# Seven quadrant products in place of eight in a second square layer: tiles 13 to 15 of a feed-forward and state-space kernel

## Chip, cores and metric

One core of one Trainium2 chip. The metric is the device time of one execution in microseconds, the median of the runs taken: 1422.49 us of 3 runs (1422.36 to 1422.56) for the kernel before. Lower is better.

## The reference, cut to what matters

`x` is 4 x 1024 tokens of 256 features. The feed-forward part runs twice, once before and once after the state-space part (a long convolution by transforms, an exact GELU and a projection):

```python
def ffn(x):                                     # weights are ternary: -1, 0, 1
    h = silu(tlin(x, w1_w, w1_s)) * tlin(x, w2_w, w2_s)      # 256 -> 1024
    h = gelu(tlin(h, h1_w, h1_s), approximate=False)         # 1024 -> 1024
    h = gelu(tlin(h, h2_w, h2_s), approximate=False)         # 1024 -> 1024
    return tlin(h, w3_w, w3_s)                               # 1024 -> 256
x = x + 0.5 * ffn(layernorm(x))
x = x + state_space(layernorm(x))
x = x + 0.5 * ffn(layernorm(x))
```

`tlin(x, w, s)` is `x @ w.T * s`, with one scale per output feature.

## The kernel before, in words

**Tiles.** The tokens go in tiles T of 512 (`TOK`); 8 tiles are the first feed-forward, T = 8 to 15 the second (`ALL` = 16). A hidden activation is [128 partitions, `KH` = 8 blocks, 512 tokens]; block k holds 128 of the 1024 features. An fp32 activation goes into TensorE as two fp32r parts, a rounded high part and the rest, so each product is made twice, with the same weight block, and summed in PSUM: exact enough for fp32, since the ternary weights are exact.

**Stages of one tile.** Steps are numbered k = 0 to 23 (`PER_U`). k = 0 to 7 (called m): layer one. `layer_one` (L1382 on) makes two products of 4 matmuls, into banks 2(m%2) and 2(m%2)+1; ScalarE's `hidden` (L498, L511) takes the SiLU of the first into one of three slots of `act_o`; VectorE's `gate` (L1246) multiplies it with the second product from PSUM, ScalarE's `gated_high` (L518) rounds the high part and VectorE's `gated_low` (L1251) makes the low part, into `hid_a_hi` and `hid_a_lo`. The second product of m waits for gate(m-2) (`s_gate`), as it overwrites the bank. k = 8 to 15: first square layer, `product` (L1362) with 16 matmuls of 512 columns a block, h1 by `hid_a`, into bank k%4. The first of these blocks waits for each low part (`s_glo`) as it comes to it. ScalarE takes the GELU (L511), VectorE's `split` (L1258, L1260) makes high and low parts in `hid_b_hi`, `hid_b_lo`. k = 16 to 23: second square layer, the same with h2, from `hid_b` into `hid_a`. Then the transposes of the next tile's normalised input (L1338), `layer_three` with the tokens as stationary operand and w3 (256 columns) moving, 64 matmuls (L1451), or `layer_three_last` (L1464) for tile 15, which lets VectorE and the stores follow one block of 128 tokens after the other. VectorE scales and adds (L1318, L1322; L1326, L1328 in the last tile).

**Order.** Every engine has its own instruction stream, written out in this order and tied by semaphores; there is no scheduler. Beside a step k each engine does other work where the schedule says so: `prepare` (taps of the convolution, tiles 0 to 3), `spectral` (the convolution, tiles 4 to 12), `norms` (the layer norm of the next tile; k = 12 and 13 in tiles 13 to 15). The convolution's buffers `zb`, `wb`, `fb`, `tt`, `ks` (from offset Z0) are used last in tile 12; its last batch of `x2` is stored from `wb` at the start of tile 13 (`store_batch`). SyncE issues all DMAs. `load_next` loads the next tile into `gz` after the last low part of layer one, `load_residual` the residual into `xin`.

**Branch.** Should a weight not fit fp32r, another path with fp32 is taken: in tile 0 VectorE ors all weights' bits (L1224), folds and sums them, and TensorE's queue loads the result (`flag`, L1608) and branches over two copies of the whole program. Five blocks of tile 0 are made ahead of the branch (`hidden_ahead`, L1434, L1436) but for their last matmul, which stands behind it (`hidden_end`, L1440).

**Alignment.** Weights and activations start on lines of 512 bytes, w3 64 bytes ahead of one:

```python
LAST += (LINE - 64 - base - LAST) % LINE
w3, FRONT = zone(LAST, ("w3", [P, KH, D], F32R))
```

## Time and profile before

| what | value |
|---|---|
| median of 3 runs | 1422.49 us (1422.36 to 1422.56) |
| profiled execution: span from first to last instruction | 1420.9 us |
| TensorE matmul busy | 1415.5 us (100%) |
| TensorE weight load busy (beside it) | 1164.5 us (82%) |
| VectorE busy | 986.1 us (69%) |
| ScalarE busy | 478.9 us (34%) |
| GpSimd busy | 48.8 us (3%) |
| DMA | 80.28 MB, mean 56 GB/s |
| granted TensorE clock | 1.00 (2.4 GHz) |
| chain that ended last | TensorE 97%, of it L1362 80%, L1451 8% |

How to read it: the span is one profiled execution, its rest to the median (1.6 us) is start and end outside the instructions. A share is that engine's busy time over the span. Matmuls are pipelined: one of 512 columns is listed with 390 ns, but the next starts 227 ns later, so the pace is read from where rows start and not from their lengths. In the timeline a row is: start, length, engine, line, operation, output <- inputs, count, and in brackets how long the engine was idle before it and what released it.

### The profile page before, as it was taken

To read this page: it belongs to the slowest core of one execution; us is meant where nothing else is said; L and a number is where in the kernel's file an instruction comes from. 1 tells how busy PE (TensorE), PEld (TensorE's weight loads), DVE (VectorE), ACT (ScalarE), POOL (GpSimd) and SP (SyncE) were. 2 spreads that over 40 slices of the span, in tenths; PEclk is the share of its full clock that TensorE was granted. 3 is DMA by queue.
4 is the path that set the end of the run, shared out by engine and by line. 5 is a ranking of instruction groups with operands and counts; after the bars stand their busy time and mean duration, and the time that the engine had idled before them with its cause. 6 is when DMAs were issued, how large, how long until landed. Compare 5 with 4: busy or idle time off the path is not lost.

```text
span 1420.9 us, 17300 instructions
## 1 busy us (share of the span) xinstructions
PE 1415.5 (100%) x6923; PEld 1164.5 (82%) x6923; DVE 986.1 (69%) x1742; ACT 478.9 (34%) x724; POOL 48.8 (3%) x43
## 2 busy tenths in 40 slices
PE   9999999999999999999999999999999999999999
PEld 4888888888878888788787888878878788888887
DVE  7877778675878888758888577784777755354433
ACT  5524342523425124232232332422424223141321
POOL 0000000000000000010000100001000010000000
PEclk9999999999999999999999999999999999999999
DMA  9001000012023111131210312112120112010000
GB/s 365 23 5 40 16 30 30 19 42 67 35 76 145 49 58 60 42 104 60 75 60 12 134 45 74 43 33 100 60 74 15 60 41 74 1 45 0 30 1 16
DMA packets 54434, 80.28 MB, mean 56 GB/s; under 512 B 2768, under 2 KB 46160, under 8 KB 53072
## 3 DMA queue, kind: packets, MB, share of 16 engines
q1 hardware_dynamic: 54352, 79.15, 16.4%
q8 instruction: 56, 0.92, 0.3%
q14 instruction: 26, 0.21, 0.0%
HBM read 57.12 MB, written 22.02 MB: 56 GB/s over the span
## 4 chain that ended last, share of the span: by engine, by line
PE 97%; issue 1%; DMA 1%; DVE 0%; SPq 0%
PE ps L1362 80%; PE ps L1451 8%; PE ps L1502 3%; PE ps L1555 2%; PE ps L1338 1%; PE ps L1434 1%; DMA raws<-in_weights 1%; PE ps L1436 1%; PE ps L1496 1%; PE ps L1497 1%; PE ps L1464 1%; PE ps L1545 0%; PE ps L1479 0%; DVE hid_a_lo L1251 0%; SPq L320 0%
## 5 line engine op out<-in xcount | busy, mean ns | idle before, releaser
L511 ACT ACTIVATE act_o<-ps,scales 128x512 f32<-128x512 f32 x384 | 264.5, 689 | 858.8 <-PE ps L1362 856.8
L1362 PE MATMUL ps<-hid_b_hi,h 128*128 128x512 f32 x1024 | 401.4, 392 | 0.0
L1362 PE MATMUL ps<-hid_b_lo,h 128*128 128x512 f32 x1024 | 398.6, 389 | 0.0
L1362 PE MATMUL ps<-hid_a_hi,h 128*128 128x512 f32 x984 | 386.9, 393 | 0.0
L1362 PE MATMUL ps<-hid_a_lo,h 128*128 128x512 f32 x984 | 383.0, 389 | 0.0
L1362 PEld LDWEIGHTS ps<-hid_b_hi,h 128*128 128x128 f32 x1024 | 192.2, 188 | 41.2 <-issue 1.2
L1362 PEld LDWEIGHTS ps<-hid_b_lo,h 128*128 128x128 f32 x1024 | 192.2, 188 | 40.7 <-issue 1.2
L1362 PEld LDWEIGHTS ps<-hid_a_hi,h 128*128 128x128 f32 x984 | 184.7, 188 | 40.5 <-issue 2.2
L1362 PEld LDWEIGHTS ps<-hid_a_lo,h 128*128 128x128 f32 x984 | 184.7, 188 | 40.2 <-issue 2.2
L1362 PE MATMUL ps<-hid_b_hi,w 128*128 128x512 f32 x480 | 187.2, 390 | 0.0
L1362 PE MATMUL ps<-hid_b_lo,w 128*128 128x512 f32 x480 | 186.8, 389 | 0.0
L1258 DVE CAST hid_b_hi<-act_o 128x512 fp32r<-128x512 f32 x128 | 54.4, 425 | 133.5 <-ACT act_o L511 132.8
L1258 DVE CAST hid_a_hi<-act_o 128x512 fp32r<-128x512 f32 x128 | 56.6, 442 | 126.7 <-ACT act_o L511 126.4
L1246 DVE SCALAR_TENSOR_TENSOR gz<-ps,scales,act_o 128x512 f32<-128x512 f32 x128 | 96.0, 750 | 47.0 <-PE ps L1362 44.4
L1451 PE MATMUL ps<-w,hid_a_hi 128*128 128x256 f32 x480 | 111.3, 279 | 0.0
L1451 PE MATMUL ps<-w,hid_a_lo 128*128 128x256 f32 x480 | 110.0, 277 | 0.0
L1362 PEld LDWEIGHTS ps<-hid_b_hi,w 128*128 128x128 f32 x480 | 90.1, 188 | 18.6 <-DVE gz L1318 0.3
L1362 PEld LDWEIGHTS ps<-hid_b_lo,w 128*128 128x128 f32 x480 | 90.1, 188 | 18.2
L1260 DVE TENSOR_TENSOR hid_b_lo<-act_o,hid_b_hi 128x512 fp32r<-128x512 f32 x128 | 88.7, 693 | 4.4
L1260 DVE TENSOR_TENSOR hid_a_lo<-act_o,hid_a_hi 128x512 fp32r<-128x512 f32 x128 | 88.6, 692 | 4.4
L1451 PEld LDWEIGHTS ps<-w,hid_a_lo 128*128 128x128 f32 x480 | 90.2, 188 | 0.0
L1451 PEld LDWEIGHTS ps<-w,hid_a_hi 128*128 128x128 f32 x480 | 90.2, 188 | 0.0
(275 smaller groups left out, 1277.6 us busy)
## 6 DMA issues: line engine op xcount, KB each, us to landing
ks<-k_d SPq DMA_DIRECT2D x32, 512.0 KB, 3.8
raws<-in_weights SPq DMA_DIRECT2D x9, 1024.0 KB, 13.7
xin<-in_x SPq DMA_DIRECT2D x8, 512.0 KB, 3.8
x_d<-xin SPq DMA_DIRECT2D x8, 512.0 KB, 2.8
z_d<-xin SPq DMA_DIRECT2D x8, 512.0 KB, 2.8
zb<-z_d SPq DMA_DIRECT2D x8, 512.0 KB, 4.9
wb<-x_d SPq DMA_DIRECT2D x8, 512.0 KB, 4.2
x_d<-wb SPq DMA_DIRECT2D x8, 512.0 KB, 3.5
```

The source lines that it names most:

```text
L511: A(act_o[:, k % ACT_SLOTS], bank(source), func, scale=scale).then_inc(s_act, 1)
L1246: V.scalar_tensor_tensor(gated[:, m % 2], bank(2 * (m % 2) + 1), scales[:, 1, m:m + 1], act_o[:, m % ACT_SLOTS], ALU.mult, ALU.mult).then_ ...
L1258: V.tensor_copy(hi[:, k % KH], source).then_inc(s_hi, 1)
L1260: V.tensor_tensor(lo[:, k % KH], source, hi[:, k % KH].bitcast(F32), ALU.subtract).then_inc(s_split, 1)
L1338: last = nc.tensor.transpose(ps[:, k, j * P:(j + 1) * P], gz[:, j, k * P:(k + 1) * P], ident[:, :])
L1362: last = MM(o, weight[:, k, cols].bitcast(dt), part[:, k].bitcast(dt), start=(k == 0 and i == 0), stop=(k == n - 1 and i == len(act_) - 1))
L1434: MM(bank(bank_of(0, k)), weight[:, kk, cols], hi[:, kk], start=kk == 0, stop=False)
L1436: MM(bank(bank_of(0, k)), weight[:, kk, cols], lo[:, kk], start=False, stop=False)
L1451: last = MM(o, part[:, k, j * P:(j + 1) * P].bitcast(dt), w3[:, k].bitcast(dt), start=(k == 0 and i == 0), stop=(k == KH - 1 and i == 1))
L1464: last = MM(ps[:, 4 + j, 0:D], part[:, k, j * P:(j + 1) * P].bitcast(dt), w3[:, k].bitcast(dt), start=(k == 0 and i == 0), stop=(k == KH - ...
L1502: last = MM(bank(o), tables[:, table_], flat(x), start=True, stop=True)
L1555: last = MM(o, ga[:, k, u * P:(u + 1) * P], wt[:, k], start=(k == 0), stop=(k == KD - 1))
```

## The change

In tiles 13 to 15 (`seven(T)`) the second square layer is made by Winograd's form of Strassen's scheme: the matrix is taken as 2 x 2 quadrants (even and odd input blocks; output features 0 to 511 and 512 to 1023), the activation as 2 x 2 as well (even and odd blocks; tokens 0 to 255, `NEAR`, and 256 to 511, `FAR`), and seven products of half size with sums before and after take the place of eight. A product for one pair of output blocks is 16 matmuls of 256 columns (`square_product`); two groups g of seven make the layer (`seven_products`).

- The sums of the activation (T1 to T4) are made by VectorE in the first square layer as the GELUs come (`even_block`, `odd_block`); the high parts, and copies of the plain quadrants, by ScalarE (`operands_high`). They stand in `back` (the convolution's buffers), `front` (over w1 and w2, from 64 bytes ahead of them) and `alone` (over z's parts, on a line). `back` and `front` start 64 bytes ahead of a line.
- The sums of products that are shared go through PSUM: ScalarE copies the first product to bank 3 and the fifth into SBUF, VectorE adds them to banks 2 and 1 (`first_sum`, `second_sum`). ScalarE's `quadrant` takes the GELU of two blocks by 256 tokens, and makes the high part; VectorE's `quadrant_low` the low one.
- Since `front` overwrites w1 and w2, these are loaded again from a scratch in DRAM (issued on ScalarE's queue in `quadrant`) before the next tile, whose layer one waits for it (`s_rw`). The scratch is written in tile 11, 2 MB from DRAM to DRAM, on SyncE's queue.
- The sums of the matrix's quadrants are made once, by VectorE in tile 13's layer one (`sums_of_weights` with k < 5), and are placed by DMAs on ScalarE's queue over `hid_b`, which these tiles don't use otherwise, and over the quadrant A21 of h2 (`place_sum`). Their bits are ored and folded at k = 5 to 13, summed by one small matmul after k = 14 in tile 13, and a second flag is made; ahead of tile 13's second layer TensorE's queue loads it (`s_flag_2`) and branches anew.
- Layer three takes the blocks in the order in which the quadrants are ready; in the last tile it now finishes each block of 128 tokens before the next.
- Small ones: `flag` and `expo` move behind the norm's buffers; in tile 0 two waits of `hidden_ahead` change places; `make_table` has a wait on `s_factor` more.

The diff, cut to its core:

```diff
...
+        front, _ = zone(FRONT - LEAD, ("front", [P, 2, 4, 2, HALF], F32R))
...
+        AT = Z0 + (LINE - LEAD) % LINE
+        back, BITS = zone(AT, ("back", [P, 4, 4, 2, HALF], F32R))
...
+                if T == SEVEN_FROM - 2:
+                    for c in range(FRONT_CHUNKS):
+                        sp.dma_start(w_d[:, chunk(c)], a["weights"][:, chunk(c)]).then_inc(s_front, 16)
...
+            def place_sum(n):
+                act.wait_ge(s_spare, 2 * n + 2)
...
+                    issue_sum(n, A21, raw_s3[:, :])
...
+            def operands_high(T, k):
+                q, slot = (k - KH) // 2, act_o[:, k % ACT_SLOTS]
+                act.wait_ge(s_act, at_u(T, k))
+                if k % 2 == 0:
+                    A(alone(q, 0), slot[:, FAR], ACT.Copy).then_inc(s_hi_a, 1)
+                else:
+                    staging_read(act, T, q)
+                    A(back[:, q, B22:B21 + 1, 0], slot.rearrange("p (h t) -> p h t", h=2), ACT.Copy).then_inc(s_hi_b, 1)
+                    act.wait_ge(s_split, at_split(T, k - 1))
+                    A(back[:, q, T1:T3 + 1, 0], back_f[:, q, T1:T3 + 1, 1], ACT.Copy).then_inc(s_hi_t, 1)
+                    act.wait_ge(s_t4, at_pair(T, q))
+                    A(front[:, :, q, 0], front_f[:, :, q, 1], ACT.Copy).then_inc(s_hi_u, 1)
+            def copy_first_product(T, g):
+                act.wait_ge(s_p1, at_block_pair(T, g))
+                act.wait_ge(s_act, at_u(T, 2 * KH + 4 * g - 1))
+                A(bank(3), bank(0), ACT.Copy).then_inc(s_p1c, 1)
+            def copy_fifth_product(T, g):
+                act.wait_ge(s_p5, at_block_pair(T, g))
+                A(fifth, bank(1).rearrange("p (m t) -> p m t", m=2), ACT.Copy).then_inc(s_p5c, 1)
+            def quadrant(T, k):
+                g, c = divmod(k - 2 * KH, 4)
+                if c == 0:
+                    copy_first_product(T, g)
+                    copy_fifth_product(T, g)
+                first, tokens = 2 * g + (0, 4, 0, 4)[c], (FAR, NEAR, NEAR, FAR)[c]
+                act.wait_ge(s_u, at_u(T, k))
+                if c == 1:
+                    act.wait_ge(s_sum2, at_block_pair(T, g))
+                act.wait_ge(s_split, at_split(T, k - ACT_SLOTS))
+                slot = act_o[:, k % ACT_SLOTS].rearrange("p (m t) -> p m t", m=2)
+                for i in range(2):
+                    last = A(slot[:, i], bank(c)[:, i * HALF:(i + 1) * HALF], ACT.Gelu,
+                             scale=scales[:, 3, first + i:first + i + 1])
+                last.then_inc(s_act, 1)
+                act.wait_ge(s_act, at_u(T, k))
+                A(hid_a_hi[:, first:first + 2, tokens], slot, ACT.Copy).then_inc(s_chi, 1)
+                if g and T + 1 < ALL:
+                    if c == 0:
+                        issue(flat_of(w2), w_d[:, chunk(1)], s_rw)
+                    if c == 3:
+                        issue(flat_of(w1), w_d[:, chunk(0)], s_rw)
...
+            def even_block(T, k):
+                q, slot = (k - KH) // 2, act_o[:, k % ACT_SLOTS]
+                dve.wait_ge(s_act, at_u(T, k))
+                staging_read(dve, T, q)
+                V.tensor_tensor(back_f[:, q, T1, 1], slot[:, NEAR], slot[:, FAR], ALU.subtract).then_inc(s_t1, 1)
+                dve.wait_ge(s_hi_a, at_pair(T, q))
+                V.tensor_tensor(alone(q, 1), slot[:, FAR], alone(q, 0).bitcast(F32),
+                                ALU.subtract).then_inc(s_lo_a, 1)
+            def odd_block(T, k):
+                q, n = (k - KH) // 2, at_pair(T, (k - KH) // 2)
+                even, slot = act_o[:, (k - 1) % ACT_SLOTS], act_o[:, k % ACT_SLOTS]
+                dve.wait_ge(s_act, at_u(T, k))
+                V.tensor_tensor(back_f[:, q, T3, 1], slot[:, NEAR], even[:, NEAR], ALU.subtract).then_inc(s_split, 1)
+                dve.wait_ge(s_t1, n)
+                V.tensor_tensor(front_f[:, T2, q, 1], slot[:, NEAR], back_f[:, q, T1, 1], ALU.subtract).then_inc(s_t2, 1)
+                dve.wait_ge(s_t2, n)
+                V.tensor_tensor(front_f[:, T4, q, 1], slot[:, FAR], front_f[:, T2, q, 1], ALU.subtract).then_inc(s_t4, 1)
+                dve.wait_ge(s_hi_t, n)
+                V.tensor_tensor(back[:, q, T1:T3 + 1, 1], back_f[:, q, T1:T3 + 1, 1],
+                                back[:, q, T1:T3 + 1, 0].bitcast(F32), ALU.subtract).then_inc(s_lo_t, 1)
+                dve.wait_ge(s_hi_u, n)
+                V.tensor_tensor(front[:, :, q, 1], front_f[:, :, q, 1],
+                                front[:, :, q, 0].bitcast(F32), ALU.subtract).then_inc(s_lo_u, 1)
+                dve.wait_ge(s_hi_b, n)
+                V.tensor_tensor(back[:, q, B22:B21 + 1, 1], slot.rearrange("p (h t) -> p h t", h=2),
+                                back[:, q, B22:B21 + 1, 0].bitcast(F32), ALU.subtract).then_inc(s_split, 1)
...
+            def first_sum(T, g):
+                dve.wait_ge(s_p6, at_block_pair(T, g))
+                if g:
+                    dve.wait_ge(s_act, at_u(T, 2 * KH + 2))
+                dve.wait_ge(s_p5c, at_block_pair(T, g))
+                V.tensor_tensor(both_of(2), both_of(3), fifth, ALU.add).then_inc(s_sum1, 1)
+            def second_sum(T, g):
+                dve.wait_ge(s_u, at_u(T, 2 * KH + 4 * g + 1))
+                V.tensor_tensor(both_of(1), both_of(3), fifth, ALU.add).then_inc(s_sum2, 1)
...
+            def sums_of_weights(T, k):
+                def sums(first, n=1):
+                    for step in range(first, first + n):
+                        if step == 0:
+                            dve.wait_ge(s_pj, B)
+                        if step == 2:
+                            dve.wait_ge(s_x2st, 32 * B)
+                        if step:
+                            dve.wait_ge(s_spare, step)
+                        part = slice(step % 2 * 2, step % 2 * 2 + 2)
+                        out, a_, b_, op = ((raw_1, A21, A22, ALU.add), (raw_2, raw_1, A11, ALU.subtract),
+                                           (raw_4, A12, raw_2, ALU.subtract), (raw_s3, A11, A21, ALU.subtract))[step // 2]
+                        V.tensor_tensor(out[:, part], a_[:, part], b_[:, part], op).then_inc(s_spare, 1)
...
+                def join_bits(first, n=1):
...
+                        dve.wait_ge(s_spare, 7 + i)
+                        V.tensor_tensor(both, words(0) if i == 1 else both, words(i), ALU.bitwise_or).then_inc(s_spare, 1)
...
+                if k < 5:
+                    sums((0, 2, 4, 5, 7)[k], (2, 2, 1, 2, 1)[k])
+                if 5 <= k < 11:
+                    join_bits((1, 3, 4, 5, 6, 7)[k - 5], 2 if k == 5 else 1)
...
+                if k == 13:
+                    dve.wait_ge(s_spare, 18)
+                    V.tensor_reduce(top, bits[:, 0:256], AX_X, ALU.max).then_inc(s_top, 1)
...
+            def second_flag():
+                dve.wait_ge(s_topsum, 1)
+                V.tensor_copy(flag_2[0:1, :], ps[0:1, 4, 0:1]).then_inc(s_spare, 1)
+                dve.wait_ge(s_spare, 19)
+                V.tensor_tensor(flag_2[0:1, :], flag_2[0:1, :], flag[0:1, :], ALU.add).then_inc(s_flag_2, 1)
...
                     first_inverses()
-                for k in range(KH, PER_U):
...
+                def beside(k):
+                    sums_of_weights(T, k)
                     prepare(T, k)
                     spectral(T, k)
                     norms(T, k)
+                for k in range(KH, 2 * KH if seven(T) else PER_U):
+                    if not seven(T):
+                        split(T, k)
+                    elif k % 2 == 0:
+                        even_block(T, k)
+                    else:
+                        odd_block(T, k)
+                    if T == SEVEN_FROM and k == KH + 6:
+                        second_flag()
+                    beside(k)
+                if seven(T):
+                    for g in range(2):
+                        k = 2 * KH + 4 * g
+                        beside(k)
+                        first_sum(T, g)
+                        beside(k + 1)
+                        second_sum(T, g)
+                        quadrant_low(T, k)
+                        quadrant_low(T, k + 1)
+                        beside(k + 2)
...
                     pe.wait_ge(s_zlo, T)
+                    if seven(T):
+                        pe.wait_ge(s_rw, 32 * (T - SEVEN_FROM))
                 elif m == 1:
...
+            def order_of_blocks(T, j):
+                return (0, 1, 4, 5, 6, 7, 2, 3) if seven(T) and j < 2 else range(KH)
...
+            def square_product(o, weight, operand, begin, dt, ready=None):
+                for q in range(4):
+                    if ready:
+                        ready(q)
+                    for part in range(2):
+                        for i in range(2):
+                            last = MM(bank(o)[:, i * HALF:(i + 1) * HALF], weight(q, i).bitcast(dt),
+                                      operand(q, part).bitcast(dt), start=begin and q == i == part == 0,
+                                      stop=q == 3 and part == 1, skip_group_check=True)
+                return last
+            def seven_products(T, g, dt):
+                n = at_block_pair(T, g)
+                at = lambda low, i: slice(low * TOK + (2 * g + i) * P, low * TOK + (2 * g + i + 1) * P)
+                even = lambda low: lambda q, i: h2[:, 2 * q, at(low, i)]
+                odd = lambda low: lambda q, i: h2[:, 2 * q + 1, at(low, i)]
+                summed = lambda s: lambda q, i: sum_row(s, q)[:, at(0, i)]
+                of = lambda operands, n: lambda q, part: (operands[:, n, q, part] if operands is front else operands[:, q, n, part])
+                k = 2 * KH + 4 * g
+                def since(done):
+                    return (lambda q: pe.wait_ge(done, at_pair(T, q))) if g == 0 else None
+                between(T, k)
+                pe.wait_ge(s_act, at_u(T, KH + 4) if g == 0 else at_u(T, 2 * KH))
+                square_product(0, even(0), alone, True, dt, since(s_lo_a)).then_inc(s_p1, 1)
+                pe.wait_ge(s_act, at_u(T, KH + 5) if g == 0 else at_u(T, 2 * KH + 1))
+                if T == SEVEN_FROM and g == 0:
+                    pe.wait_ge(s_sum_ld[0], 16)
+                square_product(1, summed(0), of(back, T1), True, dt, since(s_lo_t)).then_inc(s_p5, 1)
+                pe.wait_ge(s_p1c, n)
+                if T == SEVEN_FROM and g == 0:
+                    pe.wait_ge(s_sum_ld[1], 32)
+                square_product(3, summed(1), of(front, T2), False, dt, since(s_lo_u)).then_inc(s_p6, 1)
+                between(T, k + 1)
+                square_product(0, odd(0), of(back, B21), False, dt,
+                               (lambda q: pe.wait_ge(s_split, at_split(T, KH + 2 * q + 1))) if g == 0 else None
+                               ).then_inc(s_u, 1)
+                pe.wait_ge(s_sum1, n)
+                if T == SEVEN_FROM and g == 0:
+                    pe.wait_ge(s_sum_ld[3], 16)
+                square_product(3, even(1), of(back, T3), False, dt).then_inc(s_u, 1)
+                between(T, k + 2)
+                if T == SEVEN_FROM and g == 0:
+                    pe.wait_ge(s_sum_ld[2], 16)
+                square_product(2, summed(2), of(back, B22), False, dt).then_inc(s_u, 1)
+                between(T, k + 3)
+                pe.wait_ge(s_sum2, n)
+                square_product(3, odd(1), of(front, T4), False, dt).then_inc(s_u, 1)
...
+                    hidden(T, k, dt)
+                    if T == SEVEN_FROM and k == KH + 6:
+                        pe.wait_ge(s_top, 1)
+                        MM(ps[0:1, 4, 0:1], top, ones, start=True, stop=True).then_inc(s_topsum, 1)
...
+                feed_forward(range(SEVEN_FROM), F32R, AHEAD, from_=None)
+                two_layers(SEVEN_FROM, F32R)
             with pe.Else():
...
+                feed_forward(range(SEVEN_FROM), F32, from_=None)
+                two_layers(SEVEN_FROM, F32)
+            pe.wait_ge(s_flag_2, 1)
+            long_sums = pe.value_load(flag_2[0:1, 0:1], min_val=0, max_val=2 * 0xFFF * P)
+            with pe.If(long_sums == 0):
+                feed_forward(range(SEVEN_FROM, ALL), F32R, from_=SEVEN_FROM)
+            with pe.Else():
+                feed_forward(range(SEVEN_FROM, ALL), F32, from_=SEVEN_FROM)
...
```

## Rows read from the trace of the kernel before

**Rows 1.** The page: busy time (share) and count of an engine; a group of weight loads.

```profile
PE 1415.5 (100%) x6923; PEld 1164.5 (82%) x6923; DVE 986.1 (69%) x1742; ACT 478.9 (34%) x724; POOL 48.8 (3%) x43
...
L1451 PEld LDWEIGHTS ps<-w,hid_a_lo 128*128 128x128 f32 x480 | 90.2, 188 | 0.0
```

**Rows 2.** The chain of waits in order of time: start us, us, what.

```profile
1176.38 72.56 PE ps L1362 x320
1249.82 7.28 PE ps L1451 x64
```

**Rows 3.** Timeline of TensorE: layer one of tile 13 starts; its first square layer starts.

```profile
1176.22 0.39 PE L1362 MATMUL ps<-hid_b_hi,w 128*128 128x512 f32 x1
...
1190.74 0.39 PE L1362 MATMUL ps<-hid_a_hi,h 128*128 128x512 f32 x1
```

**Rows 4.** Timeline of VectorE, layer one of tile 13.

```profile
1179.04 0.75 DVE L1246 SCALAR_TENSOR_TENSOR gz<-ps,scales,act_o 128x512 f32<-128x512 f32 x1
1180.12 0.75 DVE L1246 SCALAR_TENSOR_TENSOR gz<-ps,scales,act_o 128x512 f32<-128x512 f32 x1 [0.33 <-PE ps L1362]
1180.79 0.68 DVE L1251 TENSOR_TENSOR hid_a_lo<-gz,hid_a_hi 128x512 fp32r<-128x512 f32 x1
...
1191.67 1.48 DVE L1251 TENSOR_TENSOR hid_a_lo<-gz,hid_a_hi 128x512 fp32r<-128x512 f32 x2
```

**Rows 5.** Timeline of VectorE, tile 0: gate, low part, check of 2048 words.

```profile
27.95 0.74 DVE L1246 SCALAR_TENSOR_TENSOR gz<-ps,scales,act_o 128x512 f32<-128x512 f32 x1
28.61 0.68 DVE L1251 TENSOR_TENSOR hid_a_lo<-gz,hid_a_hi 128x512 fp32r<-128x512 f32 x1
29.21 2.28 DVE L1224 TENSOR_TENSOR low<-low,raws 128x2048 int32<-128x2048 int32 x1
31.41 0.74 DVE L1246 SCALAR_TENSOR_TENSOR gz<-ps,scales,act_o 128x512 f32<-128x512 f32 x1
```

**Rows 6.** Groups by line and shape, 1155 to 1421 us, VectorE: busy us, mean ns | idle.

```profile
L1260 DVE TENSOR_TENSOR hid_b_lo<-act_o,hid_b_hi 128x512 fp32r<-128x512 f32 x24 | 16.6, 693 | 0.8
...
L1258 DVE CAST hid_b_hi<-act_o 128x512 fp32r<-128x512 f32 x24 | 10.2, 427 | 51.9 <-ACT act_o L511 51.9
...
L1322 DVE TENSOR_TENSOR xin<-xin,gz 128x1024 f32<-128x1024 f32 x3 | 3.7, 1225 | 0.1
...
L886 DVE BATCH_NORM_STATS2 stats<-gz 128x6 f32<-128x256 f32 x8 | 2.8, 411 | 0.0
...
L1328 DVE TENSOR_TENSOR xin<-xin,gz 128x256 f32<-128x256 f32 x4 | 1.7, 425 | 0.1
```

**Rows 7.** Groups by line and shape, whole span, ScalarE.

```profile
L511 ACT ACTIVATE act_o<-ps,scales 128x512 f32<-128x512 f32 x384 | 264.5, 689 | 858.8 <-PE ps L1362 856.8 <-PE ps L1440 1.4 <-DVE hid_b_lo L1260 0.6
L518 ACT ACTIVATE hid_a_hi<-gz 128x512 fp32r<-128x512 f32 x128 | 80.1, 625 | 13.0 <-DVE gz L1246 12.9
```

**Rows 8.** Instructions that touch the flag: duration ns, start us.

```profile
L1295 DVE CAST flag<-ps x1: 147/147/147, 51.4 to 51.4; 1x1 int32<-1x1 f32 x1
...
L1608 PEldq TENSOR_LOAD <-flag x1: 492/492/492, 51.6 to 51.6; - x1
```

**Rows 9.** Timeline of TensorE around the branch of tile 0.

```profile
52.93 1.30 PE L1440 MATMUL ps<-hid_a_lo,h 128*128 128x512 f32 x5
...
54.07 0.39 PE L1362 MATMUL ps<-hid_a_hi,h 128*128 128x512 f32 x1
```

**Rows 10.** DMA issues: KB each, median us from issue to landing.

```profile
raws<-in_weights SPq DMA_DIRECT2D x9, 1024.0 KB, 13.7
...
x_d<-wb SPq DMA_DIRECT2D x8, 512.0 KB, 3.5
...
t_d<-wb SPq DMA_DIRECT2D x1, 1024.0 KB, 3.8
...
ident<-in_ident SPq DMA_DIRECT2D x1, 64.0 KB, 3.8
```

**Rows 11.** Stretches: us, busy us by engine, granted clock, DMA share, GB/s.

```profile
0.00:6.00 6.00, 4.41 (x6) 1.85 (x6) 2.86 (x15) 1.49 (x2) 1.08 (x8) 1.00 0.57 171
```

190 lines of the change are left out of this document (150 added, 40 removed).

## The prediction

> **What bounds the kernel now.** I read the page's busy shares first: TensorE is busy 1415.5 of 1420.9 us [rows 1], so the time changes only by what TensorE executes and by what makes it wait. The chain of waits in order of time shows that nothing ended later beside it: layer one and both square layers of tile 13 are 320 matmuls in one piece of 72.56 us, layer three is 64 in 7.28 us [rows 2]. That gives the two prices: 72.56 / 320 = 0.2267 us for 512 columns, 7.28 / 64 = 0.1137 us for 256 columns, half within 1%, though each narrow one too has a weight load of its own. Then I read tile 13 from TensorE's own rows: layer one starts at 1176.22 and the first square layer at 1190.74 [rows 3], so eight blocks m take 1.81 us each. The last view is VectorE's timeline of the same stretch: gate(m) and the low half of the block before fill 1.27 us of each 1.81 [rows 4]. Layer one is the one stage where VectorE has hardly any room.
>
> **What is removed.** A second square layer is 128 matmuls of 512 columns, 128 x 0.2267 = 29.0 us. Seven products in two groups are 2 x 7 x 16 = 224 of 256 columns, 224 x 0.1137 = 25.5 us by layer three's price [rows 2]. That is 3.5 us a tile, **10.6 us for three**. The shape, the fresh weights each time and the 64 bytes off a line are layer three's own; only the `alone` operand (32 of the 224) starts on a line, which no 256-column row in fp32r shows. Bounds for such a matmul: 0.1137, and 0.188, the length of a weight load, were nothing of it hidden [rows 1]; 96 of them in three tiles would then cost 7.1 us. I take 0.1137, the row that differs only in the start; and nothing gained, since no operand is shorter.
>
> **Tile 13, layer one: the sums on VectorE.** `sums_of_weights` puts eight sums of 128x1024 at m = 0 to 4 (2, 2, 1, 2, 1) and four ors of the same width at m = 5, 6, 7 (2, 1, 1) between gate(m) and gate(m+1). One is 1.225 us by the 128x1024 add, in steady issue a little less: the 2048-wide check holds VectorE from 29.21 to 31.41, so half of it is about 1.14; chained to the one before by a semaphore it is 1.27 [rows 5, 6]. Twelve are 4 x 2.41 (pairs at m = 0, 1, 3, 5) + 4 x 1.14 = 14.2 us. From gate(0) at 1179.04 to the end of the last low half at 1193.15 the stretch is 14.1 us; gates (0.66 to the next start) and low halves (0.60) fill 10.1 of it, so 4.0 us is idle [rows 4, 5]. VectorE ends layer one 14.2 - 4.0 = **10.2 us later**. Who waits: TensorE's second product of block m overwrites the bank that gate(m-2) reads, and block k = 8 of the square layer takes the low halves one by one. It needs the last one at 1190.74 + 14 x 0.2267 = 1193.91, 0.76 after it is ready now. So TensorE stalls 10.2 - 0.7 = **9.5 us**, in about seven gaps of 0.4 to 2.8 us. ScalarE's copies and the placing DMAs have room; the store that step 2 awaits is issued before this stage and lands 3.5 us later [rows 10], while step 2 starts 7 us into it.
>
> **Tile 13, first square layer.** One block is 16 x 0.2267 = 3.63 us. A pair costs VectorE two halves and three narrow differences (0.42 each) and three wide low parts (0.69): an odd block takes 3.3 us from the GELU's end, an even one 1.0, 4.3 of 7.25 [rows 6]; ScalarE has two GELUs of 0.69 and 2.3 us of copies [rows 7]. Both fit. In tile 13 ors, folds and a norm (eight narrow operations of at most 0.42 and small ones: some 3.6) stand there as well. VectorE starts block 13 about 0.3 late, ends it 3.3 us later and the maximum 0.4 after that; TensorE waits for it (`s_top`) behind block 14, which ends 3.6 us after block 13, while the GELU of 13 ends 0.85 after it. Late by 0.85 + 0.3 + 3.3 + 0.4 - 3.6 = **1.3 us** (bounds 0 and 2.7, the whole norm in the way).
>
> **The branch.** Before the second layer TensorE's queue waits for `s_flag_2`, loads a register and branches, now also from the end of one long block over the other. Today's load takes 0.49 us at 51.6; matmuls queued before it run till 52.93, and the first behind the branch follows without a gap, so 1.3 us of queued work hid load and branch [rows 8, 9]. The new one has block 15 in front of it, but the flag comes only some 2.5 us after that block begins and the jump goes over thousands of instructions. Its fetch is in no row; the nearest is a DMA of 64 KB, which lands in 3.8 us [rows 10]. Bounds: 0 (all under block 15) and 0.49 + 2 x 3.8 = 8.1. I take **1.0**, nearer to the row of the same branch.
> The Trainium skill (Runtime: NRT & Kernel Launch, Instruction fetch mechanics) says that a taken branch to a target outside the fetched pages stalls for a fetch. The trace has no far jump, so it neither agrees nor disagrees; the rule speaks for the upper bound.
>
> **Second layer, each of tiles 13 to 15.** A product is 1.82 us. From the end of block 15: its GELU ends at about 0.9, T1 and T3 have their low parts at 2.9, needed at 1.8 + 1.4 = 3.2; ScalarE copies the first product to bank 3 by 3.6, needed at 3.6 (I add **0.1 a tile, 0.3**); the low parts for T2 come at 3.6, needed at 5.0, B21 at 4.3, needed at 6.8. The two PSUM sums (0.7 each) have a product of 1.8 in front of TensorE's need [rows 6, 7]. If one of these covers went, the tile would lose its 0.1 to 1 us there twice.
>
> **Behind the layer.** The last quadrant (two narrow GELUs, copy, low part) is ready 2.4 us after the last product, and layer three asks for it after two of its four token blocks and the transposes, 5 us. w2 and w1 are loaded again, 1 MB each, from ScalarE's queue; w1 is issued 1.7 us after the last product, and 1 MB lands in 3.8 us alone and 13.7 when nine are queued [rows 10]. It is alone: ready at 5.5 to 7, needed at 8.1, cost 0. Queued behind that issue on ScalarE are the table load and z's high part, done by 5. The 2 MB copy into the scratch in tile 11 sits on SP's queue behind that tile's last load and ahead of nothing before tile 12; 2 MB at the 13.7 us that the queued ones took is well inside that; hidden. In tile 15 layer three takes its blocks whole, 64 matmuls as now, and the tail of mult, add and store stays; 0. The reordered waits in tile 0 and the wait in `make_table` are met when reached; 0.
>
> **Sum.** -10.6 + 9.5 + 1.3 + 1.0 + 0.3 = +1.5 us. The profiled span is 1420.9; the median is 1422.49, 1.6 outside the span, which stays. 1422.49 + 1.5 = **1424.0 us**.
>
> **Rivals.**
> 1. *The sums are cheap.* Were the wide adds to run at the speed of the cast (0.43 for 512 columns) and not of the subtraction (0.69) [rows 6], twelve would take 8.6, the stall would be 3.9, and the result 1418.4: faster. Against it: every two-operand row in this trace, integers included, is on the slow line. Chance 0.13, with all else that could make the stall small.
> 2. *The far jump is not covered* (slower). TensorE drains behind block 15 of tile 13 and waits for instructions. It decides once fetch and load last over the 1 to 2 us that block 15 still covers. At the upper bound, 8.1 in place of 1.0: 1431; with one fetch, 0.49 + 3.8: 1427.3. Chance 0.14.
> 3. *The granted clock falls in tile 13* (slower). The clock is 1.00, the 2.4 GHz level, everywhere, and even in the first 6 us with TensorE busy only 4.41 [rows 11]. Here it would be about half idle for 25 us. A fall in layer one itself costs little, VectorE being the bound; but each square-layer block at 1.2 GHz costs 3.63 more: one gives 1427.6, two 1431.3. Chance 0.12. The Trainium skill (TensorE: Matmul & The Clock Gate, The HAM clock gate) says that activity releases and idleness restores the throttle; no gap here is as long as a whole block, and no row shows a fall.
> 4. *It does not do what it says: the narrow form is no cheaper.* If a product's matmul took 29.0 / 224 = 0.130, the 10.6 would be gone: 1434.6. Layer three's rows speak against it; only `alone` could differ. Chance 0.07.
> The forecast keeps 0.54.
>
> **How the numbers follow.** About 0.2% (2.8 us) is what a measurement of this kernel can tell from no change, so "same" is 1419.6 to 1425.3. The forecast's own bounds are 1421 to 1427: of its 0.54 I give 0.44 to same, 0.09 to slower, 0.01 to faster. Rival 1: 0.10 faster, 0.03 same. Rivals 2 and 3: 0.03 same, 0.23 slower. Rival 4: slower. Faster 0.11, same 0.50, slower 0.39. The range 1419.0 to 1430.0 leaves out most of rival 1, rival 4 and the upper ends of 2 and 3, some 0.2.
>
> **What the profile after would show.** Layer one of tile 13 from its first matmul to the first of block 8 takes about 21 us in place of 14.5, and VectorE is nearly full in it; TensorE's waits there name VectorE's gz. The 112 matmuls of one group stand 0.1137 apart, tiles 14 and 15 are each 3.5 us shorter and without gaps. A gap of 1 to 2 us stands ahead of block 15, and one of about 1 ahead of the first product. Wrong if layer one of tile 13 has no gaps, if the products of `alone` are wider apart than the others, if the clock leaves 1.00, or if tile 14 begins by waiting for w1.

## The result, and the profile after

The changed kernel takes 1425.57 us (median; 1423.93 to 1427.94) beside 1422.49 for the kernel before: a ratio of 1.002 with an interval of 1.001 to 1.0029. A second set gave 1424.18, ratio 1.0012 (1.0002 to 1.0021). The forecast was 1424.0. The profiled execution is one of 1425.57 us; its span is 1423.8, before 1420.9. e1, e4 and e6 each hold one execution of over 2000 us in a slow state; it counts in the medians given (without it e1 1416.44, e4 1426.8, e6 1424.14) and not in the ratios.

The chain of waits in order of time (start us, us, what), from block 15 of tile 13 to the end:

```profile
1226.55 0.19 PE ps L1926 x2
1226.74 3.87 PE ps L1635 x16
1230.61 0.39 issue
1231.00 25.84 PE ps L1750 x224
1256.84 0.88 PE ps L1611 x8
1257.72 7.54 PE ps L1739 x64
1265.26 43.52 PE ps L1635 x192
1308.78 25.61 PE ps L1750 x224
1334.39 0.87 PE ps L1611 x8
1335.26 7.27 PE ps L1739 x64
1342.53 43.53 PE ps L1635 x192
1386.07 25.61 PE ps L1750 x224
...
1419.43 0.42 DVE xin L1601
```

The 224 matmuls of a second square layer stand as one piece of 25.61 us where 128 x 0.2267 = 29.0 stood [rows 2], and tiles 14 and 15 have no gap: from one layer one to the next (1265.26 to 1342.53) is 77.27 us, where before it was 43.53 + 29.0 + 0.88 + 7.28 = 80.69. That is **3.42 us less a tile**.

Tile 13 pays it back. TensorE's timeline there, the rows with a gap (start, us, what, idle before and its releaser):

```profile
1182.84 0.50 PE L1635 MATMUL ps<-hid_b_hi,w 128*128 128x512 f32 x1 [0.16 <-DVE gz L1393]
1186.49 0.50 PE L1635 MATMUL ps<-hid_b_hi,w 128*128 128x512 f32 x1 [1.53 <-DVE gz L1393]
...
1198.59 0.49 PE L1635 MATMUL ps<-hid_a_hi,h 128*128 128x512 f32 x1 [2.45 <-DVE gz L1393]
1203.32 0.50 PE L1635 MATMUL ps<-hid_a_hi,h 128*128 128x512 f32 x1 [1.00 <-DVE hid_a_lo L1398]
1226.54 0.19 PE L1926 MATMUL ps<-single 128*1 128x1 f32 x2 [0.74 <-DVE single L1502]
```

(These rows are of the second profiled execution of the same kernel, e6, span 1422.3; in the first they stand within 0.01 us of these.) The matmul at 1198.59 is the first of block 8, the one at 1203.32 its fifteenth, the first to need the last low half; block 9 starts at 1203.89, where before it was 1194.37: **9.5 us later**. The seven gaps of the list come to 7.2 us of it. The rest is in the matmuls beside them: one is listed 0.16 us longer than its pace, which hides that much of each gap, and the matmuls behind a gap take some 0.15 us more in sum than their pace.

VectorE's timeline of the same stretch, in the first execution, says why:

```profile
1178.98 0.75 DVE L1393 SCALAR_TENSOR_TENSOR gz<-ps,scales,act_o 128x512 f32<-128x512 f32 x1
1179.64 2.48 DVE L1474 TENSOR_TENSOR raw<-h 128x1024 f32<-128x1024 f32 x2
1182.04 0.75 DVE L1393 SCALAR_TENSOR_TENSOR gz<-ps,scales,act_o 128x512 f32<-128x512 f32 x1
1182.70 0.68 DVE L1398 TENSOR_TENSOR hid_a_lo<-gz,hid_a_hi 128x512 fp32r<-128x512 f32 x1
...
1201.45 1.22 DVE L1481 TENSOR_TENSOR bits<-bits,raw 128x1024 int32<-128x1024 int32 x1
1202.58 0.68 DVE L1398 TENSOR_TENSOR hid_a_lo<-gz,hid_a_hi 128x512 fp32r<-128x512 f32 x1
```

Every row begins where the one before ends: VectorE is full from 1179 to 1203.26 and finishes the last low half 10.1 us later than before [rows 4]. By windows, from the first matmul of layer one to that at 1203.32 it is 27.2 us, of which TensorE works 19.96 and VectorE 26.6. The page's shares hide all of this: PE 1408.5 (99%) in place of 1415.5, a drop of 7.0 us that does not show in the time.

The last line of the sum is the end of the kernel. VectorE's last add starts at 1419.43, 1.06 us later than before (1418.37); in the second execution 1.33. The other 1.8 us of the span's 2.9 lie behind it. SyncE's waits (us in total, times, longest), first of the changed kernel, then of the kernel before:

```profile
SPq L190 <- DMA out_x<-xin: 3.1, 1, 3.1
```

```profile
SPq L169 <- DMA out_x<-xin: 1.3, 1, 1.3
```

The last store of 128 KB took 3.5 us to land in place of 1.7.

### The profile page after: what moved, and what is told of

It reads as the page before. It is cut to its first block, busy times and chain, and to the rows that moved or that the text cites. A ratio compares the mean times of both kernels' runs of the same rounds, so it can differ in the third digit from the quotient of the medians.

```text
span 1423.8 us, 18099 instructions
## 1 busy us (share of the span) xinstructions
PE 1408.5 (99%) x7213; PEld 1168.7 (82%) x7213; DVE 1022.1 (72%) x1799; ACT 530.5 (37%) x832; POOL 48.6 (3%) x43
## 4 chain that ended last, share of the span: by engine, by line
PE 97%; DVE 2%; issue 1%; DMA 0%; ACT 0%; POOL 0%; DVEq 0%; ACTq 0%
PE ps L1635 74%; PE ps L1739 8%; PE ps L1750 5%; PE ps L1837 3%; PE ps L1890 2%; PE ps L1611 1%; PE ps L1710 1%; PE ps L1712 1%; PE ps L1831 1%; PE ps L1832 1%; PE ps L1804 1%; PE ps L1880 0%; DVE gz L1393 0%; PE ps L1814 0%; DVE hid_a_lo L1398 0%
## 5 line engine op out<-in xcount | busy, mean ns | idle before, releaser
L582 ACT ACTIVATE act_o<-ps,scales 128x512 f32<-128x512 f32 x360 | 247.9, 689 | 763.9 <-PE ps L1635 760.9
L1635 PE MATMUL ps<-hid_b_hi,h 128*128 128x512 f32 x832 | 326.7, 393 | 0.0
L1635 PE MATMUL ps<-hid_b_lo,h 128*128 128x512 f32 x832 | 323.9, 389 | 0.0
L1635 PEld LDWEIGHTS ps<-hid_b_hi,h 128*128 128x128 f32 x832 | 156.2, 188 | 33.7 <-issue 1.2
L1635 PEld LDWEIGHTS ps<-hid_b_lo,h 128*128 128x128 f32 x832 | 156.2, 188 | 33.2 <-issue 1.2
L1405 DVE CAST hid_b_hi<-act_o 128x512 fp32r<-128x512 f32 x104 | 44.2, 425 | 81.8 <-ACT act_o L582 81.4
L1405 DVE CAST hid_a_hi<-act_o 128x512 fp32r<-128x512 f32 x104 | 46.3, 445 | 67.4 <-ACT act_o L582 67.1
L656 ACT ACTIVATE hid_a_hi<-gz 128x512 fp32r<-128x512 f32 x128 | 80.1, 626 | 23.4 <-DVE gz L1393 23.3
L1398 DVE TENSOR_TENSOR hid_a_lo<-gz,hid_a_hi 128x512 fp32r<-128x512 f32 x128 | 87.3, 682 | 1.4
```

What stands on the lines that cost most here:

```text
L582: A(act_o[:, k % ACT_SLOTS], bank(source), func, scale=scale).then_inc(s_act, 1)
L656: A(hid_a_hi[:, m], gated[:, m % 2], ACT.Copy).then_inc(s_ghi, 1)
L1398: V.tensor_tensor(hid_a_lo[:, m], gated[:, m % 2], hid_a_hi[:, m].bitcast(F32), ALU.subtract).then_inc(s_glo, 1)
L1405: V.tensor_copy(hi[:, k % KH], source).then_inc(s_hi, 1)
L1635: last = MM(o, weight[:, k, cols].bitcast(dt), part[:, k].bitcast(dt), start=(k == 0 and i == 0), stop=(k == n - 1 and i == len(act_) - 1))
```

## The experiments

**e6: the change itself, once more.** 

> The changed kernel itself, to have a second profile of it and more runs beside the others on this chip. Theory (its runs differ by the clock in tile 13 and by the landing of the last store, and not by anything in the other tiles): about 1425.5, spans of 1422 to 1426 with the lowest clocks at the longest; in the profile all gaps of tile 13 within 0.1 us of those of the first profile, and whatever is more stands in tile 13 at a clock below 1.00 or behind the last matmul. Rival: the difference is spread over all tiles.


1424.18 us (from 1423.51). Its last store landed in time: the wait above was 1.4, and the span 1422.3. So the first profile's tail is not in every execution of the change. TensorE's rows agree with the first to 0.02 us up to the end of block 15 of tile 13; the first product stands 0.27 later, see e8. What was expected of the clock did not come: the mean granted clocks of 0.998 go with spans of 1421.9 to 1424.0 and those of 0.999 with 1421.7 to 1423.9.

**e1: no sums.** 

> The changed kernel without the eight sums of h2's quadrants and without the ors and folds of their bits: each is a 128x1 memset of VectorE in the same place with the same semaphores, and the DMAs place plain quadrants of h2 where the sums would stand. The numbers of tiles 13 to 15 are therefore not the reference's; TensorE's, ScalarE's and the DMAs' work is the same. Theory (the sums on VectorE hold TensorE in tile 13): all gaps of layer one go (9.5 us in the profile after) and the one ahead of block 15 (1.0 us) shrinks to under 0.3, so the span falls from 1423.8 by 10 to 10.5 to about 1413.5, and the time to 1415 to 1416, 0.5% under the kernel before. Rival (the stalls are only moved: something else in tile 13, the placing DMAs or ScalarE's copies, is next late): gaps stay, and the time stays above 1419.

```
- V.tensor_tensor(out[:, part], a_[:, part], b_[:, part], op).then_inc(s_spare, 1)
+ V.memset(count[:, :], 0.0).then_inc(s_spare, 1)
```

The ors and folds are replaced in the same way, and the DMAs place plain quadrants of the matrix, so the products of the second layer are not the reference's. 1416.51 us, ratio 0.9947 (0.9929 to 0.9966). The chain has one piece where the gaps were, and one that stays:

```profile
1176.25 36.30 PE ps L1635 x160
...
1216.51 0.34 DVE single L1502
...
1216.89 0.19 PE ps L1926 x2
1217.08 3.88 PE ps L1635 x16
...
1221.70 25.85 PE ps L1750 x224
```

Layer one and the square layer run through at 0.2267 a matmul, and the first product starts at 1221.70 in place of 1231.00: **the sums cost 9.3 us** by that row. Block 9 starts 9.65 earlier (1194.24), so all of it is in layer one and in block 8; the branch took 0.36 more in this execution. The 0.7 us ahead of block 15 stays without them. It comes from the odd block's own chain, which the rows above end: GELU, three differences, low parts, the reduction. That part of the expectation missed.

**e2: operands on a line.** 

> The changed kernel with LEAD = 0: the operands front and back start on a line of 512 bytes, as alone does already; nothing else is changed. In the profile after, the 16 matmuls of an alone product take 1.92 us (0.120 each) and those of back and front 1.82 (0.1137 each). Theory (the start on the line is what makes alone's matmuls longer): the other six products of a group take 0.120 too, a tile's 224 take 26.8 in place of 25.6 us, and three tiles are 3.6 us longer: span about 1427.4, time about 1429. Rival (it is the switch between stages, or the partner of the weight load, and not the line): 25.6 us a tile as now, time 1425 to 1426.

```
-LEAD = 64
+LEAD = 0
```

1427.52 us, 1.0038 (1.0025 to 1.0051), where some 1429 was expected. The second layer of tile 14 in the chain:

```profile
1310.00 26.88 PE ps L1750 x224
```

26.88 / 224 = 0.1200 us each, 1.27 us more a tile than 25.61, 3.8 in three; VectorE's last add starts at 1423.19, 3.8 later than in the first profile of the change and 3.5 later than in e6. In the change itself the `alone` product, the one that lies on a line, shows the same: 16 matmuls in 1.92 us (1308.61 to 1310.53), 0.120 each, where the other products take 1.81 to 1.83. Off the line it is (25.61 - 32 x 0.12) / 192 = 0.1134, so the line costs 0.0066 us a matmul.

**e3 and e10: seven products from tile 14, the sums beside tile 13's square layers.** 

> Seven products in tiles 14 and 15 alone. The eight sums are made one at a time beside k = 8 to 15 of tile 13, the ors beside k = 16 to 21 and the folds at 22 and 23, where VectorE is idle for 2.5 of each 3.6 us; they are placed in tile 14's layer one, as they were in tile 13's. Theory: no gap in a layer one and none ahead of block 15; two tiles gain 3.4 us each, and only the 0.6 us at the branch is paid: span 1420.9 - 6.8 + 0.6 = 1414.7, time about 1416.3 (0.44% under before). Rival (sums beside the square layers make VectorE late too, above all with the norm at k = 12 and 13): TensorE waits for the split of tile 13's blocks, and the time is 1418 or more.

```
-SEVEN_FROM = 13
+SEVEN_FROM = 14
-                if T != SEVEN_FROM:
+                if T != SEVEN_FROM - 1:
                     return
-                if k < 5:
-                    sums((0, 2, 4, 5, 7)[k], (2, 2, 1, 2, 1)[k])
+                if KH <= k < 2 * KH:
+                    sums(k - KH)
...
```

1418.27 us, 0.9966 (0.9953 to 0.9978); again in e10, 1416.69, 0.9958 (0.9944 to 0.9972). The chain of e3:

```profile
1256.57 39.91 PE ps L1634 x176
...
1296.59 3.87 PE ps L1634 x16
1300.46 0.46 issue
1300.92 25.85 PE ps L1749 x224
```

The eight sums, now beside tile 13's first square layer, and all seven ors and the folds, beside its second, cost nothing there: 176 matmuls at 0.2267 with no gap, and only the branch is left. Two tiles' gain of 3.4 each, less the branch, stays: VectorE's last add starts at 1411.81, 6.6 us earlier than before.

**e4: the sums on GpSimd.** 

> Seven products in tiles 13 to 15 as in the change, but the eight sums are made by GpSimd, which is idle there; VectorE keeps the ors, at m = 3 and 5 and k = 8 to 12, and the folds at 13. GpSimd needs 2.4 us for a 128x1024 operation by the bias rows of before, so 19 us, ready some 22 us into tile 13, long before they are needed. Theory: layer one loses at most 1 us (two ors of 1.2 in 4.0 us of idle time), the wait ahead of block 15 becomes about 2.2 us, branch 0.6: span 1420.9 - 10.3 + 3.8 = 1414.4, time about 1416. Rival (GpSimd and VectorE hold each other up when both work on SBUF: while GpSimd added the bias in tile 12, a cast of VectorE took 0.97 in place of 0.43 us): VectorE's rows of layer one are longer while GpSimd works, TensorE stalls by several us, and the time is 1419 or more.

```
+            def sums_of_weights():
+                for step in range(8):
...
+                    G.tensor_tensor(out[:, part], a_[:, part], b_[:, part], op).then_inc(s_spare, 1)
```

1427.17 us, 1.0032 (1.0019 to 1.0045): the eight sums left VectorE and the time did not fall. The edit also moves ors: two stay in layer one, five stand beside blocks 8 to 12 and the folds behind block 13. VectorE's timeline while GpSimd adds:

```profile
1180.24 0.75 DVE L1409 SCALAR_TENSOR_TENSOR gz<-ps,scales,act_o 128x512 f32<-128x512 f32 x1 [0.33 <-PE ps L1651]
...
1185.47 2.02 DVE L1414 TENSOR_TENSOR hid_a_lo<-gz,hid_a_hi 128x512 fp32r<-128x512 f32 x1
1187.40 3.38 DVE L1499 TENSOR_TENSOR bits<-raw 128x1024 int32<-128x1024 int32 x1
...
1198.06 0.67 DVE L1414 TENSOR_TENSOR hid_a_lo<-gz,hid_a_hi 128x512 fp32r<-128x512 f32 x1
```

The subtraction with two operands in SBUF takes 2.02 us in place of 0.67, an or 3.38 in place of 1.22; the gate, which reads PSUM, keeps its 0.75. The Trainium skill (SBUF — State Buffer, Who interferes with whom) says that a VectorE instruction with two SBUF inputs contends with a GpSimd instruction that reads SBUF, as the second input comes through a read interface that they share. The trace agrees by these rows, and GpSimd's own sums go from 2.4 us to 2.8 to 3.2. Block 9 starts at 1201.95, 7.6 us later than before where the change is 9.5 later, though VectorE has two wide operations in layer one in place of twelve. TensorE waits 3.20 us in layer one as well, and the clock is 0.50 behind that too. Then the maximum, which the later ors and folds hold back, made TensorE wait 3.2 us ahead of block 15, and behind that block 15 ran partly at half clock:

```profile
1227.23 5.50 PE ps L1651 x16
```

Sixteen matmuls in 5.50 us in place of 3.87.

**e5: four ors at once.** 

> The changed kernel with the four ors of layer one all at m = 7 (in the change: two at 5, one at 6, one at 7); VectorE does the same work in the stage and ends it at the same time, but TensorE's last waits, about 1.5, 2.5 and 1 us, become one or two of together 5 us just ahead of and in block 8. Theory (the granted clock is a cost of its own: where TensorE waits for over some 3 us the clock drops to 1.2 GHz, as in the profile of the sums on GpSimd, where it fell with gaps of 3.2 us ahead of it, and the matmuls then stand 0.427 us apart): the clock is below 1.00 in most runs, blocks 8 and 9 run partly at 0.43 us a matmul, and the time is 2 to 4 us above the change: 1427 to 1429. Rival (only VectorE's end counts): blocks 8 and 9 run at 0.227 and the time is that of the change, 1424 to 1425.6.

```
-                if 5 <= k < 11:
-                    join_bits((1, 3, 4, 5, 6, 7)[k - 5], 2 if k == 5 else 1)
+                if k == 7:
+                    join_bits(1, 4)
+                if 8 <= k < 11:
+                    join_bits(k - 3)
```

1428.06 us, 1.0036 (1.0022 to 1.005). VectorE's work is the same, and the fifteenth matmul of block 8 starts at 1203.94, 0.6 later than in the change. What is new is the length of one wait. TensorE's timeline, and the windows behind it (stretch, us, busy and count of PE, PEld, DVE, ACT, POOL, granted clock, DMA share, GB/s):

```profile
1203.94 0.80 PE L1637 MATMUL ps<-hid_a_hi,h 128*128 128x512 f32 x1 [4.15 <-DVE hid_a_lo L1398]
...
1206.24 0.63 PE L1637 MATMUL ps<-hid_a_lo,h 128*128 128x512 f32 x1
1206.66 0.63 PE L1637 MATMUL ps<-hid_a_hi,h 128*128 128x512 f32 x1
...
1211.22 0.39 PE L1637 MATMUL ps<-hid_a_lo,h 128*128 128x512 f32 x1
```

```profile
1206.00:1208.00 2.00, 2.00 (x7) 1.52 (x6) 1.90 (x3) 0.33 (x1) 0.00 (x0) 0.50 1.08 381
1208.00:1210.00 2.00, 2.00 (x6) 1.60 (x5) 0.00 (x0) 0.00 (x0) 0.00 (x0) 0.50 0.19 65
1210.00:1212.00 2.00, 2.00 (x10) 1.58 (x9) 0.09 (x1) 0.78 (x2) 0.00 (x0) 0.99 0.00 0
```

After the wait of 4.15 us the granted clock is 0.50, the 1.2 GHz level; thirteen matmuls stand 0.43 apart (1203.94 to 1209.65) and then 0.23 again: 13 x 0.2 = 2.7 us. With the 0.6 that is 3.3 of the 3.5 us by which the first product starts later. The theory that a fall of the clock is a cost of its own held. Its figure of some 3 us for the wait did not: in e2, e8 and e9 the clock falls with a wait of 2.46, in e12 behind one of 2.26.

**e8: one branch.** 

> The changed kernel without the second branch: TensorE goes from the square layer of tile 13 into the seven products without waiting for the second flag, loading it or jumping (the flag is still made, and what follows from it in another input is left out). Theory: the gap of 0.55 us ahead of the first product of tile 13 goes, the one ahead of block 15 stays at 1.0, and the span is 0.4 to 0.6 us shorter than a profile of the change with the same tail. Rival (the wait is for T1's or alone's parts and not for the branch): the gap stays.

```
+                feed_forward(range(ALL), F32R, AHEAD, from_=None)
...
-            pe.wait_ge(s_flag_2, 1)
-            long_sums = pe.value_load(flag_2[0:1, 0:1], min_val=0, max_val=2 * 0xFFF * P)
...
```

The choice by the second flag is left out. 1423.16 us, ratio 1.0004 (0.9995 to 1.0013), 1.0 below e6 on the same chip. Its timeline across the place, that of the change, and the chain of the change's second profile, e6, with the load of the flag in the first:

```profile
1229.96 0.39 PE L1635 MATMUL ps<-hid_a_lo,h 128*128 128x512 f32 x1
1230.18 1.00 PE L1750 MATMUL ps<-alone_hi,h 128*128 128x256 f32 x7
```

```profile
1230.22 0.39 PE L1635 MATMUL ps<-hid_a_lo,h 128*128 128x512 f32 x1
1231.00 1.18 PE L1750 MATMUL ps<-alone_hi,h 128*128 128x256 f32 x8 [0.39 <-issue]
```

```profile
1230.59 0.68 issue
1231.27 25.85 PE ps L1750 x224
```

```profile
L1974 PEldq TENSOR_LOAD <-flags x1: 322/322/322, 1230.1 to 1230.1; - x1
```

0.22 between the two without the branch; with it 0.78 in the first profile (**0.56 us for the branch**) and 1.07 in e6 (1230.20 to 1231.27, **0.85**), so the medians' difference of 1.0 has its row for the most part. Of all kernels that branch behind an undisturbed block 15, the first profile is the cheapest: 0.83 in e2 and e5, 1.14 in e1, 1.24 in e9, 0.84 to 1.00 in e3, e7, e10 and e11 (in e4 and e12 the slow block 15 hides it). The branch costs 0.56 to 1.02 us. In every one the first product stands 0.9 to 1.0 us behind the start of the flag's load, and that load starts within 0.4 us of block 15's last matmul, though in the first profile VectorE has the flag ready at 1228.7 and the load starts at 1230.1. Why it starts no sooner no row tells.

**e7, e9 and e11: the old order of layer three in the last tile.** 

> The kernel with seven products from tile 14 on (e3_from_14), with layer three of the last tile in the order of the kernel before: seven blocks for tokens 0 to 255 first, then the last block of each, then the rest. Before, 1.6 to 2.1 us passed from VectorE's last add to the end of the span; in the profiles of the change, of e1_no_sums and of e3_from_14 it was 3.6 to 4.0, in those of e2_on_a_line and e4_sums_gpsimd 2.1. Theory (the order of the last stores makes one DMA engine late with the last of them): this tail is 2.1 in most runs, and the median is 1 to 1.5 us under that of e3_from_14, 1416.8. Rival (the tail varies by itself, whatever the order): the median stays at 1418.

> The change with one thing put back: in the last tile layer three goes through token blocks 0 and 1 up to block 7 first, then through the last blocks, as the kernel before did, so that the first of the four last stores come closer together and later. Theory A, the order of layer three in the last tile sets how long the last store takes to land: the time is 1.0 to 1.5 us below the change's 1424.2 to 1425.6, that is 1423.0 to 1424.2. Theory B, the long landing of the last store comes and goes by itself: no difference over 0.4 us, 1424.2 to 1425.6, and the gaps of TensorE are those of the change.

> The kernel that starts the seven products in tile 14 and makes the sums beside the square layers of tile 13, as it was run before (1418.27, 1416.84 to 1419.26). Theory A, order of the last layer three: again 1.0 to 1.3 us above the same kernel with the old order. Theory B: the two agree within 0.4 us, as TensorE's last matmul ends at the same time in both.

> The kernel that starts in tile 14 with the old order of layer three in the last tile, as it was run before (1417.12, 1416.5 to 1417.34). Theory A: 1416.8 to 1417.3 again and 1.0 to 1.3 us below the kernel with the new order. Theory B: within 0.4 us of that kernel.

```
-                for j in range(J):
-                    for n, k in enumerate(order_of_blocks(T, j)):
+                for j in range(2):
+                    steps_of(j, 0, KH - 1)
+                for j in range(J):
+                    steps_of(j, KH - 1 if j < 2 else 0, KH).then_inc(s_o, 1)
```

I thought that the new order (the blocks whole, one after the other) made the last store late. e7, which is e3 with the old order, seemed to show it: 1417.12 against e3's 1418.27. But those two ran on different chips. Side by side, e11 (old order) gave 1416.94 and e10 (new order) 1416.69; and the change with the old order, e9, 1423.94 beside e6's 1424.18 (within the range written for the first theory, but only 0.24 apart). The theory that the order alone decides fell; the one that the landing comes and goes by itself stands. In the profiled executions of all kernels the wait for the last store is 2.8 to 3.3 us in three (the change's first, e1, e3) and 1.3 to 1.4 in the eleven others, e6 and e10 among them, which are the same kernels as the first and the third. All three long ones have the new order, seven short ones have it too, and none of the four with the old order is long; so the order may still make a long landing more frequent. What makes it long is open.

**e12: the sums spread evenly.** 

> The change with its sums and ors spread more evenly: one sum of 128x1024 behind each gate of blocks 0 to 5, two at block 6, two ors at block 7, and the other five ors and the folds behind blocks 8 to 13 of the first square layer. Ten wide operations stand in layer one in place of twelve. Theory, the price of a wide operation is set by the stage it stands in: six single ones of 1.14 us and two pairs of 2.41 are 11.7 us in place of 14.2, so block 9 starts 2.5 us earlier than in the change, with no wait over 2 us; one more or and the folds come later, up to 1.5 us on the wait ahead of block 15. Total 1422.3 to 1424.5, and no fall of the clock. Rival, only the sum of VectorE's work over layer one and the square layer counts: the time stays at 1424.2 to 1425.6.

```
-                if k < 5:
-                    sums((0, 2, 4, 5, 7)[k], (2, 2, 1, 2, 1)[k])
-                if 5 <= k < 11:
-                    join_bits((1, 3, 4, 5, 6, 7)[k - 5], 2 if k == 5 else 1)
+                if k < 7:
+                    sums(k, 2 if k == 6 else 1)
+                if 7 <= k < 13:
+                    join_bits((1, 3, 4, 5, 6, 7)[k - 7], 2 if k == 7 else 1)
...
```

The placing DMAs are issued at other steps too. 1427.24 us, 1.0032 (1.002 to 1.0045): slower than either theory said. TensorE's rows, the fifteenth matmul of block 8 and the small one ahead of block 15:

```profile
1200.63 0.50 PE L1635 MATMUL ps<-hid_a_hi,h 128*128 128x512 f32 x1 [2.26 <-DVE hid_a_lo L1398]
1227.94 0.19 PE L1926 MATMUL ps<-single 128*1 128x1 f32 x2 [3.16 <-DVE single L1502]
```

The first starts 2.69 us earlier than in the change, as block 9 does, about as worked out (2.5). But the last or, both folds and the norm now stand between block 12 and the reduction, and the wait ahead of block 15 is 3.16 us in place of 0.73. The clock falls after both waits. From that matmul to the end of block 14 it is 24.15 us (1200.63 to 1224.78) in place of 22.49 (1203.32 to 1225.81), and from block 15's first matmul to the first product it is 5.36 (1228.06 to 1233.42) in place of 4.33, although the slow block now covers the branch. -2.69 + 1.66 + 2.43 + 1.03 = +2.43, which is where the first product stands: 1233.42 in place of 1231.00. Half of the theory held, the price of an operation in layer one; I had bounded the new wait at 1.5 and left out the clock behind it. The rival, no change, is as wrong. This kernel and e4 have the same wait of 3.2 us ahead of block 15, with the folds behind block 13 in both.

## Why the prediction was right, step by step

- **The gain, 3.5 a tile.** Measured 3.42 in tiles 14 and 15. A layer takes 25.61 where I had 25.47: the term that was off is `alone`, whose start on a line I had taken as free, 32 x 0.0066 = 0.2 us, less 0.06 by which the others are under 0.1137; e2 shows the effect by itself. Rival 4 had named the place and put its price far too high.
- **Layer one of tile 13, 9.5.** VectorE was to end 10.2 later; it ended 10.1 later. Block 9 begins 9.5 us later than before, and e1 gives 9.65 back there. Twelve operations of 1.14 or 2.41 a pair, less 4.0 us of idle time, less 0.7 of slack: the sum needed only rows of the kernel before. Rival 1 (cheap sums) fell with the row of 2.48 us for a pair.
- **Ahead of block 15, 1.3.** Measured 1.0 (block 14's end to block 15's start), of which 0.74 is the named wait. The reason was partly wrong: I had put 0.3 of it to the ors and folds, and e1, without them, still waits 0.7. It is the odd block's chain with the reduction behind it. The gap was to be 1 to 2 us in the profile, and is 0.7.
- **The branch, 1.0.** Measured 0.56 in the first profile, 0.85 in e6 and at most 1.02, between my bounds of 0 and 8.1 and near the lower. Rival 2 (fetches of 3.8 us) is out. The flag's load takes 0.32 us of it, so a far jump costs 0.7 us at most here. I had let block 15 cover part of load and jump; it covers next to nothing, as the load starts beside its last matmul and not when the flag is ready. The stall that the Trainium skill names (Runtime: NRT & Kernel Launch, Instruction fetch mechanics), cited in the prediction for the upper bound, does not show at that size.
- **Product into bank 3, 0.1 a tile.** Nothing: the 224 are one piece. **The reload of w1 and w2, 0.** Right: tile 14 begins without a wait.
- **Not in the sum.** In tile 13 the 224 take 25.84 and layer three 7.54, 0.5 us more than in tile 15. For the first 0.2 a row shows a slower start behind the gap; for the 0.27 in layer three (0.118 a matmul) none does. The last layer three of the kernel before took 7.55 and takes 7.27 now, 0.28 less; e9, with the old order, has 7.27 too, so it is not the order.
- **The total.** For the chain's end: 9.5 + 1.0 + 0.56 + 0.5 - 0.28 - 3 x 3.42 = +1.0 us; the row shows +1.06. With e6's branch, 0.85, it is +1.3 and the row +1.33. Forecast +1.5. So close a total is luck in part: three costs that were too high by 1.0 together (ahead of block 15, the branch, bank 3) make up for a gain that was too high by 0.3 and for 0.2 that was in no term. The median of 1425.57 is 1.6 above the forecast, that of the second set 0.2. In the first the long landing of the last store is 1.8 us of the profiled execution; how often it is there in the others no row tells, so the 1.4 us between the two sets stay open.
- **The signs of being wrong.** Layer one of tile 13, from its first matmul to the first of block 8, takes 22.4 us (expected about 21, before 14.5). Of the four signs two came: `alone` is wider apart than the others, and the clock leaves 1.00.
- **Rival 3, the clock.** Its condition came true far more often than the chance of 0.12 says, and its price did not; this is where my text was too calm. In the first two profiles of the change the clock stays at 1.00 after the wait of 2.45 us. They are the exception: the mean granted clock of the execution is below 1.000 in seven of the nine executions of the first set and in ten of the eleven of the second, and in six of 48 of the kernel before. In the first set the two of 0.997 have the longest spans (1424.8 and 1426.0). In e8, e9 and e2, which have the same gaps up to there, the fall has rows. Windows of e9:

```profile
1200.00:1202.00 2.00, 2.00 (x6) 1.55 (x5) 2.00 (x4) 0.51 (x1) 0.00 (x0) 0.50 0.01 4
1202.00:1204.00 2.00, 2.00 (x7) 1.53 (x7) 1.79 (x3) 1.61 (x3) 0.00 (x0) 0.72 0.00 0
```

Here it costs next to nothing: block 8 waits for VectorE's last low half anyway, the slow matmuls use up the 1.00 us gap at 1203.32, and from block 8 to block 15 it is 28.13 us in e8 and 28.19 in e9, beside 28.07 in the second profile of the change. That is the sentence of rival 3 that a fall in layer one costs little. Where the waits lie otherwise, as in e5 (the low half late within block 8), in e12 (there, and ahead of block 15) and in e4 (ahead of block 15), a fall costs 1.6 to 2.7 us. The Trainium skill (TensorE: Matmul & The Clock Gate, HAM oscillation — how this bites in real kernels) tells that waits between pieces of work bring the slow clock back. These traces agree for waits of 2.3 to 4.2 us, and show that one of 2.45 us, with shorter ones ahead of it, does it in some executions and not in others.

## What to carry to other kernels

Price a preparation by the stage that it is put in, not by the engine's share over the whole span: VectorE was 31% idle, yet twelve operations of 1.2 us cost 9.5 us in the one stage where it had 4 us to spare, and nothing in the square layers of e3. The fastest kernels here give up one of the three tiles for that and are 0.4% faster than the kernel before (0.9955 to 0.9966 in e3, e7, e10 and e11), and so faster than the change. Sums made early enough to keep all three tiles, beside the square layers of tile 12, were not tried. Where TensorE must wait, put the wait where another engine is the bound anyway, and charge it with the slow matmuls that may follow: 1.6 to 2.7 us here behind waits of 2.3 to 4.2 where no other engine was the bound.
